# A two-layer graph attention network: folding W2 with the source vector and spreading late scores beside the last blocks

## Chip, cores, metric

One core of a Trainium2 chip. The time is the device time of one execution in microseconds. The kernel before takes 937.47 us, the median of three runs (936.48 to 937.52).

## What is computed

The reference is two graph attention layers over 1250 nodes and 20000 edges (with self loops), a residual and a layer norm. `src` and `dst` are drawn edge lists, so the kernel builds the count matrix of edges on the chip and treats each layer as dense attention with that matrix as weight.

```python
def _gat_layer(x, src, dst, W, a_src, a_dst, bias, concat):
    h = (x @ W).reshape(N, H, C)
    al_s = einsum('nhc,hc->nh', h, a_src)
    al_d = einsum('nhc,hc->nh', h, a_dst)
    e = leaky_relu(al_s[src] + al_d[dst], 0.2)
    m = segment_max(e, dst)
    ex = exp(e - m[dst])
    alpha = ex / (segment_sum(ex, dst)[dst] + 1e-16)
    out = segment_sum(h[src] * alpha[:, :, None], dst)
    ...
h = elu(_gat_layer(x, ..., W1, as1, ad1, b1, concat=True))     # 4 heads of 512
out = _gat_layer(h, ..., W2, as2, ad2, b2, concat=False)       # 1 head, 768
return layernorm(x + out)
```

What matters here: the second layer's source score of a node is the dot product of h2 = hidden x W2 with `as2`. It is also the dot product of the hidden row with the folded vector W2 x as2. And the shift of each target needs the largest source score among its neighbours, so it needs the source scores of all nodes.

## The kernel before

Nodes are in NB = 10 blocks of B = 125. All matrix products are made of three float32r matmuls (high x high, high x low, low x high; the helper `products`, L1722 to L1728), so every operand is split into a high part (ACT, a copy) and a low part (DVE, a subtraction).

Layer one runs over four heads. A head is 20 chunks: two groups g of five target blocks, ten source blocks b each. For each chunk ACT makes relu (`act_relu`, L585), POOL adds the shift row (`pool_add`, L595), ACT makes exp (L610), DVE multiplies by counts (L617), ACT splits off the high part (L623) and DVE the low part (L632), into three slots; TensorE multiplies with the head's hx and hlo (`chunk`, L1851). In the second group of heads 0 to 2 TensorE also makes the next head's block (`make`, L1875), DVE splits it (`split_h`) and makes the masked maxima of the next head, and the next shift goes through DRAM (`store_shift`, L720, `load_grow`, L714). `make(h, b)` waits for the low split of block b - 2. Chunks are numbered through, 0 to 79 in layer one (CHUNKS = 80), 80 to 99 in layer two.

The second projection reads the hidden rows back from DRAM (`hblk`, two slots), transposes each block in two halves of eight 128-column pieces (`transpose_h`, L1840, half n of block n // 2), ACT and DVE split the transposed half (`split_hT`, L1123, L1450), and `mm_half` (L1896) makes 8 steps of six matmuls with W2p, high and low parts of W2 in SBUF. The first half is transposed behind chunk 77, the second behind mm_half(0). ACT evicts each block (`h2_out`), DVE makes its two dot products with as2 and ad2 (`scores2`, L1514), each source score goes through DRAM into the row arow2, and DVE makes the neighbour maxima of the ten target blocks in four pieces: sources 0 to 3 (`maxima2`), then 4 and 5, 6 and 7, 8 and 9 (`part_maxima2`, p = 0 to 2), ten maxima each and a merge.

After the last block the order is written out by hand: last dot products, TensorE spreads the last source score over all partitions (`spread`, L1788, a matmul with a broadcast column against the identity), ten maxima of part 2, merge, the shift of all ten blocks (`dve_shift`, L637), a spread of all target scores (drow2) in between, then the spread of the shift (gcol) in two groups, evictions of these rows, and the chunk loop of layer two, whose low and high parts have ten slots (PT2). TensorE holds the first group's sums of all five target blocks in PSUM (`piece2`, ORDER2), then waits for DVE's first two evictions (`evict2`) and takes the second group target by target. Eviction, norm and store follow block by block on DVE, POOL (rsqrt by pow) and SP. SP's queue issues every DMA, in its program order.

Of the kernel before, what the change touches and what calls it, by code (L numbers as in the profile page):

```python
# [14 lines left out]
F32 = mybir.dt.float32  # L15
# [15 lines left out]
H = 4  # L31
# [68 lines left out]
W2F = 8  # L100

# [21 lines left out]
def gat_kernel(nc, x, src, dst, W1, as1, ad1, b1, W2, as2, ad2, b2, out):  # L123
# [5 lines left out]
    s2_d = nc.dram_tensor("score2_scratch", (NB, B), F32, kind="Internal").ap()  # L129
    hid_d = nc.dram_tensor("hidden_scratch", (N, HID), F32, kind="Internal").ap()  # L130

    with ExitStack() as ctx:
# [103 lines left out]
        pbuf = sb("pbuf", [B, PR, GN], F32)  # L236

# [59 lines left out]
        cursor[0] = tail_at + HID * 4  # L297
        nbp.append(sb("nbp2", [B, NB, QW], BF16))
        cursor[0] = tail_at + 6 * N * 2
        drow2 = sb("drow2", [B, N], F32)  # L300
        pbuf2 = sb("pbuf2", [B, PR, GN], F32)
# [3 lines left out]
        grow2 = sb("grow2", [B, N], F32)  # L305
        xres += [sb(f"xres{i}", [B, D], F32) for i in range(2, GT)]
        assert cursor[0] <= tail_at + 6 * N * 2
# [10 lines left out]
        PT2 = [sb(f"PT2_{i}", [B, 2, GN], F32R) for i in range(3, PR2)] + PT2  # L318
# [88 lines left out]
        d2_sb = sem("d2_sb")  # L407
        g2_sb = sem("g2_sb")
        s2_stored = sem("s2_stored")
        ld_s2 = [sem(f"ld_s2_{i}") for i in range(QP + 1)]  # L410
        h2x_one = sem("h2x_one")
# [20 lines left out]
        h2_sb = sem("h2_sb")  # L432
        al2_done = sem("al2_done")
# [107 lines left out]
        def ht_banks(half):  # L541

            return ((6, 7), (4, 5))[half]
# [29 lines left out]
        def pslot(c):  # L573

            return pbuf[:, c % PR, :] if c < CHUNKS else pbuf2[:, c % PR, :]
# [9 lines left out]
        def act_relu(act, c):  # L585
# [5 lines left out]
            if h < H and b == 0:  # L591
                act.wait_ge(ld_drow[g], RS * (h + 1))
            act.activation(pslot(c), src[:, g * GN:(g + 1) * GN], ACT.Relu, scale=UP, bias=bias).then_inc(z_done, 1)  # L593

        def pool_add(pool, c):  # L595
# [53 lines left out]
        def _(sp):  # L649
# [136 lines left out]

            for h in range(H - 1):
# [1202 lines left out]
```

## Time and profile before

| | |
|---|---|
| median of three runs | 937.47 us |
| the profiled execution | 937.02 us |
| its span | 935.1 us |
| mean granted clock of TensorE | 0.987 |
| PE busy | 881.1 us (94%) |
| DVE busy | 602.1 us (64%) |
| ACT busy | 424.4 us (45%) |
| POOL busy | 198.1 us (21%) |
| HBM traffic | 118 GB/s over the span |

The page of the profile has the busy tenths of each engine in 40 slices of 23.4 us. From slice 9 on TensorE is at 9 or more in all slices but one: the slice from 795 to 818 us, where its busy digit is 6 and its clock digit 7. DVE is near full in layer one and in the last fifth, and at 2 to 4 during the second projection. Busy shares say which engine has room; what sets the end is read from the waits and from the times at which a stage's last steps stand.

### The profile page before, as it was taken

The numbers are of one execution on the slowest core, as the hardware profiler recorded it, in microseconds if no ns is written. First come the engines' busy times: TensorE is split into PE (matmuls) and PEld (weight loads), VectorE is DVE, ScalarE is ACT, GpSimd is POOL, SyncE is SP. The second block draws the span as 40 slices with busy tenths as digits, with TensorE's granted clock in tenths as the row PEclk, the third lists the DMA queues.
The fourth block names the chain that finished last, engine by engine and source line by source line (L and its number), as shares of the span: only waits on it lengthen the run. The fifth ranks groups of instructions, "written<-read, shape, count | busy, mean of one in ns | idle before, by whom it ended". The sixth has DMA issues, their size and how long they took to land.

```text
span 935.1 us, 15156 instructions
## 1 busy us (share of the span) xinstructions
PE 881.1 (94%) x5719; PEld 796.9 (85%) x5719; DVE 602.1 (64%) x1169; ACT 424.4 (45%) x686; POOL 198.1 (21%) x134
## 2 busy tenths in 40 slices
PE   4998879999999999999999999989999999699996
PEld 2455557799888998889988899989999999599996
DVE  9458663668873889638895488672223334497886
ACT  5456452276643866339652396661111111487300
POOL 1000000144212332124321244300000000155452
PEclk9999989999999999999999999999999999799999
DMA  8609999462548237472174243655223322400223
GB/s 298 145 14 132 178 174 159 135 211 81 177 138 239 67 103 212 112 231 78 29 214 139 68 142 117 174 166 115 72 48 70 85 48 30 102 1 2 69 84 95
DMA packets 64450, 111.18 MB, mean 119 GB/s; under 512 B 31772, under 2 KB 33464, under 8 KB 63004
## 3 DMA queue, kind: packets, MB, share of 16 engines
q1 hardware_dynamic: 64379, 110.22, 45.7%
q8 instruction: 46, 0.75, 0.4%
q14 instruction: 25, 0.20, 0.1%
HBM read 85.25 MB, written 24.94 MB: 118 GB/s over the span
## 4 chain that ended last, share of the span: by engine, by line
PE 67%; DVE 11%; issue 9%; POOL 6%; ACT 3%; DMA 2%; DVEq 1%; SPq 1%; POOLq 0%; ACTq 0%
PE ps L1726 19%; PE ps L1728 19%; PE ps L1727 19%; POOL pbuf L608 5%; PE ps L1755 3%; PE ps L1696 2%; PE ps L1847 2%; PE ps L1686 1%; DVE pbuf L621 1%; DVE h2f L1632 1%; DMA mask_scratch<-nbs 1%; DVE h2f L1606 1%; DVE vbuf L1440 1%; DMA w1f<-in_L_gnn_W 1%; DVE bnst L1623 1%
## 5 line engine op out<-in xcount | busy, mean ns | idle before, releaser
L608 POOL TENSOR_TENSOR pbuf<-pbuf,grow 125x625 f32<-125x625 f32 x100 | 169.9, 1700 | 701.2 <-ACT pbuf L593 261.1
L1726 PE MATMUL ps<-hx,PThi 125*125 125x260 f32 (+5 forms) x800 | 227.3, 284 | 3.0 <-DVE vbuf L1441 2.5
L1728 PE MATMUL ps<-hx,PTlo 125*125 125x260 f32 (+5 forms) x800 | 225.4, 282 | 0.0
L1727 PE MATMUL ps<-hlo,PThi 125*125 125x260 f32 (+4 forms) x800 | 224.9, 281 | 0.0
L1726 PEld LDWEIGHTS ps<-hx,PThi 125*125 125x125 f32 x800 | 148.7, 186 | 7.0 <-DVE vbuf L1441 2.9
L1727 PEld LDWEIGHTS ps<-hlo,PThi 125*125 125x125 f32 x800 | 149.1, 186 | 1.4
L1728 PEld LDWEIGHTS ps<-hx,PTlo 125*125 125x125 f32 x800 | 149.0, 186 | 0.0
L1726 PE MATMUL ps<-W2p,hT 128*125 128x384 f32 x320 | 109.7, 343 | 3.2 <-DVE hT L1453 1.7
L1728 PE MATMUL ps<-W2p,hT 128*125 128x384 f32 x320 | 108.1, 338 | 0.0
L1727 PE MATMUL ps<-W2p,hT 128*125 128x384 f32 x320 | 108.1, 338 | 0.0
L621 DVE SCALAR_TENSOR_TENSOR pbuf<-pbuf,counts 125x625 f32<-125x625 f32 x100 | 90.7, 907 | 25.3 <-ACT pbuf L615 25.2
L630 ACT ACTIVATE PThi<-pbuf 125x625 fp32r<-125x625 f32 x80 | 57.8, 722 | 106.1 <-PE ps L1728 57.0
L615 ACT ACTIVATE pbuf<-pbuf,s_sl 125x625 f32<-125x625 f32 x100 | 81.2, 812 | 48.9 <-POOL pbuf L608 48.8
L635 DVE TENSOR_TENSOR PTlo<-pbuf,PThi 125x625 fp32r<-125x625 f32 x80 | 77.1, 964 | 40.4 <-ACT PThi L630 40.2
L1453 DVE TENSOR_TENSOR hT<-ps,hT 128x500 fp32r<-128x500 f32 x40 | 25.2, 672 | 108.7 <-ACT hT L1129 108.7
L1726 PE MATMUL ps<-h2x,PT 125*125 125x384 f32 (+9 forms) x250 | 77.6, 310 | 6.2 <-DVE PT L635 4.2
L1129 ACT ACTIVATE hT<-ps 128x500 fp32r<-128x500 f32 x40 | 21.2, 586 | 133.0 <-PE ps L1847 133.0
L593 ACT ACTIVATE pbuf<-drow,s_up 125x625 f32<-125x625 f32 x100 | 80.2, 804 | 0.0
L1727 PE MATMUL ps<-h2lo,PT 125*125 125x384 f32 (+7 forms) x250 | 77.3, 309 | 0.0
L1728 PE MATMUL ps<-h2x,PT 125*125 125x384 f32 (+9 forms) x250 | 77.3, 309 | 0.0
L1728 PE MATMUL ps<-W1hi,xr 128*125 128x512 f32 x180 | 71.1, 395 | 0.0
L1726 PE MATMUL ps<-W1hi,xr 128*125 128x512 f32 x180 | 71.0, 395 | 0.0
(186 smaller groups left out, 1571.6 us busy)
## 6 DMA issues: line engine op xcount, KB each, us to landing
xr<-xT_scratch SPq DMA_DIRECT2D x30, 750.0 KB, 4.9
nbm<-mask_scratch SPq DMA_DIRECT2D x40, 273.4 KB
hidden_scratch<-vbuf SPq DMA_DIRECT2D x40, 224.0 KB
hblk<-hidden_scratch SPq DMA_DIRECT2D x10, 896.0 KB
xT_scratch<-xa SPq DMA_DIRECT2D x20, 375.0 KB, 11.7
w1f<-in_L_gnn_W SPq DMA_DIRECT2D x12, 512.0 KB, 9.1
w1raw<-in_L_gnn_W SPq DMA_DIRECT2D x4, 1536.0 KB, 7.9
w2raw<-in_L_gnn_W SPq DMA_DIRECT2D x14, 384.0 KB, 5.4
```

Source lines behind the costliest of these rows:

```text
L593: act.activation(pslot(c), src[:, g * GN:(g + 1) * GN], ACT.Relu, scale=UP, bias=bias).then_inc(z_done, 1)
L608: pool.tensor_tensor(pslot(c), pslot(c), src[:, g * GN:(g + 1) * GN], ALU.add).then_inc(e_done, 1)
L615: act.activation(pslot(c), pslot(c), ACT.Exp, scale=SLOPE, bias=bias).then_inc(p_done, 1)
L621: dve.scalar_tensor_tensor(pslot(c), pslot(c), 1.0, C[:, b, g * GN:(g + 1) * GN], ALU.min, ALU.mult).then_inc(pc_done, 1)
L630: act.activation(hi_slot(c), pslot(c), ACT.Copy).then_inc(pt_hi, 1)
L635: dve.tensor_tensor(lo_slot(c), pslot(c), hi_slot(c).bitcast(F32), ALU.subtract).then_inc(pt_lo, 1)
L1129: hi = act.activation(ht_part(n % 2, 0, a), PS[:, bank, 0:4 * B], ACT.Copy)
L1453: lo = dve.tensor_tensor(ht_part(n % 2, 1, a), PS[:, bank, 0:4 * B], ht_part(n % 2, 0, a).bitcast(F32), ALU.subtract)
L1726: pe.matmul(dst, ahi, bhi, start=start, stop=False, skip_group_check=shared)
L1727: pe.matmul(dst[:, 0:n], ahi, blo, start=False, stop=False, skip_group_check=shared)
L1728: return pe.matmul(dst, alo, bhi, start=False, stop=stop, skip_group_check=shared)
L1755: t = pe.matmul(win_bank(w), oh_lo[:, bass.ds(at_slot(first, i, v), 1), :].rearrange("p o n -> p (o n)"), ring[:, w % 2, v, 0:win_cols(w)] ...
```

## The change

The source scores of the last two blocks no longer come from h2. W2 x as2 is computed in layer one: sixteen row blocks of W2 are loaded into one buffer (`load_fold2`) and DVE multiplies each with as2 and sums it (FOLD2: in the second groups of heads 0, 1 and 2, chunks b = 0, 1, 5, 8, 9, in head 2 also 7). The folded vector goes to DRAM and comes back as a row in three pieces (PP: 768, 768, 512 columns); DVE makes the dots of hidden blocks 8 and 9 with it (`late_dots`), in the iterations of blocks 6 and 7, and adds them (`late_scores`).

TensorE spreads the source scores of blocks 7, 8 and 9 in the second half of block 8 (before step LATE_S = 6), so that parts 1 and 2 of the maxima and the shift of targets 0 to 4 are made beside the last two blocks. It spreads that shift in the last half (before step LATE_G = 3). The last block's h2 is evicted behind the first chunk's high split. DVE adds the shift to chunk 80 straight from PSUM; the rows of the target scores (drow2) and of the second group's shift come through DRAM. The first chunk of layer two waits for the banks piece by piece. The slots of PT2 are taken in another order, and `prow`, `nbp2` and `drow2` have other places in SBUF. ACT waits for the last maximum ahead of h2_out(8), and SP's b2row and xres loads stand behind the new row loads.

The second half of the first hidden block is transposed behind chunk 78, with the same banks as the first half, and split ahead of the last group's eviction.

```diff
+PP = ((0, D), (D, 2 * D), (2 * D, HID))
+LATE_S, LATE_G = 6, 3
+FOLD2 = tuple((h, b) for h in range(H - 1) for b in ((0, 1, 5, 8, 9) if h < H - 2 else (0, 1, 5, 7, 8, 9)))
...
+            def load_fold2(h, b):
+                if (h, b) in FOLD2:
+                    i = FOLD2.index((h, b))
+                    if i > 0:
+                        sp.wait_ge(fold2_done, i)
+                    sp.dma_start(wf2[:], W2[128 * i:128 * i + 128, :]).then_inc(ld_fold2, 16)
...
+                load_fold2(h, 0)
                 if h > 0:
                     for t in range(GT):
                         store_hid(NB * h - GT + t)
                 load_drow(h + 1, 0)
+                load_fold2(h, 1)
                 if h + 2 < H:
...
+                    load_fold2(h, (5, None, 7, None, 8)[t])
                 store_shift(h + 1)
                 load_grow(h + 1, 0)
                 load_xr(h + 1, NB - 2)
+                load_fold2(h, 9)
...
+            load_prow(2)
+            sp.wait_ge(ht_ps, 2 * NB - 2)
+            load_part(1)
+            sp.wait_ge(dot_done, 2 * len(PP) + 1)
+            load_part(2)
+            sp.wait_ge(g_stored, RS * H)
+            load_row(drow2, d2_d, 0, ld_drow[0])
+            sp.wait_ge(al2_done, 2 * NB - 2)
+            store_column(d2_d, al2[:, 1, GT:NB], 1)
+            sp.wait_ge(g_done, H + 2)
+            store_column(g2_d, gcol[:, H * NB + GT:(H + 1) * NB], 1)
+            sp.wait_ge(g_stored, RS * (H + 2))
+            load_row(drow2, d2_d, 1, ld_drow[1])
+            load_row(grow2, g2_d, 1, ld_grow[1])
...
             split_hT(0)
+            act.wait_ge(pt_lo, CHUNKS)
+            split_hT(1)
             act.wait_ge(ag, ag_at(CHUNKS - 1))
...
+                    if b == NB - 2:
+                        act.wait_ge(bc2_ps, 1)
+                        act.activation(arow2[:, (NB - 3) * B:N], PS[0:B, 6, 0:3 * B], ACT.Copy).then_inc(bc2_sb, 1)
                     split_hT(2 * b + 3)
-                h2_out(b)
+                if b == NB - 2:
+                    act.wait_ge(mx_last, QP * NB)
+                if b < NB - 1:
+                    h2_out(b)
...
             split_h2(0)
-            shift2_out(0)
-            shift2_out(1)
             act_exp(act, CHUNKS)
+            act.wait_ge(bc2_ps, 2)
+            act.activation(grow2[:, 0:CW], PS[0:B, 4, 0:CW], ACT.Copy)
+            act.activation(grow2[:, CW:GN], PS[0:B, 5, 0:B], ACT.Copy).then_inc(bc2_sb, 1)
+            act_hi(act, CHUNKS)
+            h2_out(NB - 1)
+            act.wait_ge(h2_sb, NB)
+            act_exp(act, CHUNKS + 1)
...
+                if g == 1 and (h, b) in FOLD2:
+                    i = FOLD2.index((h, b))
+                    dve.wait_ge(ld_fold2, RS + 16 * (i + 1))
+                    dve.wait_ge(fold2_done, i)
+                    dve.scalar_tensor_tensor(wf2junk[:], wf2[:], 1.0, as2row[:], ALU.mult, ALU.mult, accum_out=w2a[:, i:i + 1]).then_inc(fold2_done, 1)
...
+            def late_dots(p):
+
+                lo, hi = PP[p]
+                dve.wait_ge(ld_a2, 2 * RS + RS * (p + 1))
+                dve.wait_ge(al2_done, 2 * NB - 6 if p < 2 else 2 * NB - 4)
+                for b in (NB - 2, NB - 1):
...
+                    dve.scalar_tensor_tensor(a2junk[:, 0, 0:hi - lo], hblk[:, b % 2, lo:hi], 1.0, prow[:, 0:hi - lo], ALU.mult, ALU.mult,
+                                             accum_out=dots[:, b - NB + 2, p:p + 1]).then_inc(dot_done, 1)
...
+                split_hT(2 * b + 3)
+                if b == 8:
+                    for m in range(NB):
+                        part_maxima2(2, m)
+                    merge(2)
+                    shift2(0)
                 scores2(b)
+                if b == 6:
+                    late_dots(0)
+                if b == 7:
+                    late_dots(2)
+                    late_scores()
...
+            dve.wait_ge(z_done, CHUNKS + 1)
+            dve.wait_ge(bc2_ps, 2)
+            dve.tensor_tensor(pslot(CHUNKS)[:, 0:CW], pslot(CHUNKS)[:, 0:CW], PS[0:B, 4, 0:CW], ALU.add)
+            dve.tensor_tensor(pslot(CHUNKS)[:, CW:GN], pslot(CHUNKS)[:, CW:GN], PS[0:B, 5, 0:B], ALU.add).then_inc(e_done, 1)
+            split_h2(0)
+            dve_counts(dve, CHUNKS)
+            dve_lo(dve, CHUNKS)
+            scores2(NB - 1)
+            shift2(1)
...
-                if c == CHUNKS - 3:
-                    transpose_h(0)
+                if c in (CHUNKS - 3, CHUNKS - 2):
+                    transpose_h(c - CHUNKS + 3)
...
+                    if n == 2 * NB - 3 and k == LATE_S:
+                        pe.wait_ge(dot_done, 2 * len(PP) + 1)
+                        pe.wait_ge(ht_lo, 2 * NB - 1)
+                        spread(lambda m: al2[:, 0, m:m + 1], lambda m: (6, (m - NB + 3) * B), NB - 3, NB).then_inc(bc2_ps, 1)
+                    if n == 2 * NB - 1 and k == LATE_G:
+                        pe.wait_ge(g_done, H + 1)
+                        spread(lambda m: gcol[:, H * NB + m:H * NB + m + 1], four_from(4), 0, GT).then_inc(bc2_ps, 1)
...
                 for u, order in enumerate(ORDER2):
+                    if c == 0 and u < 2:
+                        pe.wait_ge(h2_sb, NB - 1 + u)
+                    if c == 0 and u == 2:
+                        pe.wait_ge(bc2_sb, 2)
```

## Rows read from the trace of the kernel before

**Rows 1.** Waits of TensorE from 800 us on: us in total, times, longest

```profile
PE ps L1726 <- DVE PT L635: 4.2, 1, 4.2
PE ps L1726 <- DVE h2f L1606: 2.0, 1, 2.0
```

**Rows 2.** Timeline, projection's end and chunk loop: start, length, engine, line, operation

```profile
766.64 0.95 DVE L1520 SCALAR_TENSOR_TENSOR a2junk<-h2f,a2row 125x768 bf16<-125x768 f32 x1
...
781.03 1.02 PE L1847 MATMUL ps<-ident,hblk 125*128 125x125 f32 x8
781.81 0.42 PE L1726 MATMUL ps<-W2p,hT 128*125 128x384 f32 x1
...
798.98 0.81 ACT L1167 ACTIVATE h2f<-ps 125x768 f32<-125x768 f32 x1 [15.12 <-PE ps L1728]
...
812.36 0.82 ACT L615 ACTIVATE pbuf<-pbuf,s_sl 125x625 f32<-125x625 f32 x1
...
815.38 0.80 ACT L593 ACTIVATE pbuf<-drow,s_up 125x625 f32<-125x625 f32 x1
...
815.87 0.55 PE L1726 MATMUL ps<-h2x,PT 125*125 125x256 f32 x1 [4.19 <-DVE PT L635]
...
872.19 0.80 ACT L593 ACTIVATE pbuf<-drow,s_up 125x625 f32<-125x625 f32 x1
```

**Rows 3.** Stretches: length, busy us (xcount) of each engine, PEclk, DMA share, GB/s

```profile
815.80:818.80 3.00, 2.93 (x14) 2.96 (x15) 2.38 (x3) 2.71 (x5) 1.52 (x1) 0.50 0.20 52
818.80:868.00 49.20, 49.20 (x414) 49.20 (x414) 41.67 (x39) 38.70 (x52) 25.60 (x15) 1.00 0.01 1
...
873.20:876.60 3.40, 3.40 (x11) 3.40 (x12) 2.61 (x3) 0.95 (x2) 3.40 (x2) 0.53 0.58 184
```

**Rows 4.** Timeline of TensorE: the spread of ten columns ahead of layer one

```profile
180.33 2.42 PE L1792 MATMUL ps<-ident,gcol 125*125 125x125 f32 x20 [1.04 <-DVE gcol L645]
```

**Rows 5.** Timeline of DVE: first of ten part maxima, and their merge

```profile
786.13 0.41 DVE L1545 CUSTOM_DVE_ANT_0 junk<-nbp,arow 125x250 bf16<-125x250 bf16 x1
...
790.77 0.17 DVE L1553 TENSOR_TENSOR mx<-mx,mxp 125x10 f32<-125x10 f32 x1
```

**Rows 6.** Timeline at the end: DVE's last eviction, TensorE's last matmul

```profile
927.24 0.15 DVE L1594 TENSOR_SCALAR deps<-ps 125x1 f32<-125x1 f32 x1
...
927.41 0.34 PE L1728 MATMUL ps<-h2x,PT 125*125 125x384 f32 x1
```

**Rows 7.** Timeline, layer one's end: transposes, split, eviction, first products of two halves

```profile
601.93 0.27 PE L1847 MATMUL ps<-ident,hblk 125*128 125x125 f32 x1
...
604.13 1.25 DVE L1453 TENSOR_TENSOR hT<-ps,hT 128x500 fp32r<-128x500 f32 x2
608.33 0.16 DVE L1427 TENSOR_SCALAR deps<-ps 125x2 f32<-125x2 f32 x1 [2.94 <-PE ps L1728]
...
611.63 0.44 PE L1726 MATMUL ps<-W2p,hT 128*125 128x384 f32 x1 [1.55 <-DVE vbuf L1441]
...
623.71 0.44 PE L1726 MATMUL ps<-W2p,hT 128*125 128x384 f32 x1 [1.66 <-DVE hT L1453]
```

**Rows 8.** Page's DMA issues, SP's waits, and the timeline in head 1

```profile
w2raw<-in_L_gnn_W SPq DMA_DIRECT2D x14, 384.0 KB, 5.4
...
SPq L717 <- DMA shift_scratch<-gcol: 20.6, 3, 7.5
...
402.87 0.69 DVE L1339 TENSOR_TENSOR hlo<-ps,hx 125x512 fp32r<-125x512 f32 x1 [0.38 <-ACT hx L995]
...
409.52 0.40 PE L1726 MATMUL ps<-W1hi,xr 128*125 128x512 f32 x1
```

**Rows 9.** DVE's W1 split beside POOL and alone; head 1's second group as stretch

```profile
317.98 1.79 DVE L1343 TENSOR_TENSOR W1lo<-w1raw,W1hi 128x512 fp32r<-128x512 f32 x1
...
333.95 0.68 DVE L1343 TENSOR_TENSOR W1lo<-w1raw,W1hi 128x512 fp32r<-128x512 f32 x1
...
344.00:420.00 76.00, 75.79 (x470) 67.44 (x469) 50.18 (x85) 32.37 (x49) 16.60 (x11) 1.00 0.60 171
```

More of the change, by code:

```diff
@@ L236, in gat_kernel @@
         pbuf = sb("pbuf", [B, PR, GN], F32)
+        wf2 = sb("wf2", [128, D], F32)
+        wf2junk = sb("wf2junk", [128, D], BF16)
+        w2a = sb("w2a", [128, KC], F32)
+        cursor[0] = base_attr
+        as2row = sb("as2row", [128, D], F32)
         cursor[0] = base_attr + 2 * (N * 4 + 24)
@@ L317, in gat_kernel @@
         h2lo = sb("h2lo", [B, NB, D], F32R)
-        PT2 = [sb(f"PT2_{i}", [B, 2, GN], F32R) for i in range(3, PR2)] + PT2
+        PT2 = [PT2[2], PT2[1]] + [sb(f"PT2_{i}", [B, 2, GN], F32R) for i in range(3, PR2)] + [PT2[0]]
         assert cursor[0] <= base0 + 2 * KC * D * 4
@@ L539, in h2_banks, with ht_banks @@
             return PS[0:B, 2 * s:2 * s + 2, 0:DH]
-        def ht_banks(half):
-            return ((6, 7), (4, 5))[half]
+        def ht_banks(n):
+            return (4, 5) if n % 2 and n > 1 else (6, 7)
         def ht_part(half, part, a):
@@ L810, in _ @@
                 load_grow(h + 1, 1)
+            sp.wait_ge(fold2_done, KC)
+            for lo, hi in ((0, XP), (XP, 128)):
+                sp.dma_start(w2a_d.rearrange("k p -> p k")[lo:hi, :], w2a[lo:hi, :], allow_slow_non_contiguous=True).then_inc(rows_stored, 16)
             sp.wait_ge(mk_done, H * NB)
@@ L955, in add_bias_late @@
                 pool.tensor_tensor(y[:, n, :], y[:, n, :], b2row[:], ALU.add).then_inc(yb_done, 1)
-            for c in range(CHUNKS, CHUNKS + 2 * NB):
+            pool.wait_ge(e_done, CHUNKS + 1)
+            for c in range(CHUNKS + 1, CHUNKS + 2 * NB):
                 pool_add(pool, c)
@@ L1498, in _ @@
             split_hT(0)
+            split_hT(1)
             evict_group(NG - 1)
@@ L1553, in merge, with late_scores, shift2 @@
                 dve.tensor_tensor(mx[:, lo:hi], mx[:, lo:hi], mxp[:, p * NB:(p + 1) * NB], ALU.max).then_inc(mx_all, 1)
-            for b in range(NB):
-                if b > 0 and b + 1 < NB:
+            dots = bnst[:, 0:2, 0, 0:len(PP)]
+            def late_dots(p):
[3 more added lines that the diff above has]
+                for b in (NB - 2, NB - 1):
+                    if p > 0 or b == NB - 1:
+                        dve.wait_ge(dot_done, 2 * p + b - NB + 2)
+                    if p == 0:
+                        dve.wait_ge(ld_hb[b % 2], RS * (b // 2 + 1))
+                    dve.scalar_tensor_tensor(a2junk[:, 0, 0:hi - lo], hblk[:, b % 2, lo:hi], 1.0, prow[:, 0:hi - lo], ALU.mult, ALU.mult,
+                                             accum_out=dots[:, b - NB + 2, p:p + 1]).then_inc(dot_done, 1)
+            def late_scores():
+                dve.wait_ge(dot_done, 2 * len(PP))
+                dve.tensor_reduce(al2[:, 0, NB - 2:NB], dots, AX.X, ALU.add).then_inc(dot_done, 1)
+            def shift2(g):
+                lo, hi = H * NB + g * GT, H * NB + (g + 1) * GT
+                dcol = al2[:, 1, g * GT:(g + 1) * GT]
+                dve.wait_ge(mx_all, QP)
+                dve.wait_ge(al2_done, (2 * GT, 2 * NB - 2)[g])
+                dve.scalar_tensor_tensor(mneg[:, lo:hi], mx[:, lo:hi], -1.0, dcol, ALU.mult, ALU.subtract).then_inc(m_neg, 1)
+                dve.wait_ge(m_neg, H + 1 + g)
+                dve.scalar_tensor_tensor(negm[:, lo:hi], mneg[:, lo:hi], SLOPE, mneg[:, lo:hi], ALU.mult, ALU.min).then_inc(m_sb, 1)
+                dve.wait_ge(m_sb, H + 1 + g)
+                dve.scalar_tensor_tensor(gcol[:, lo:hi], negm[:, lo:hi], 1 / SLOPE, dcol, ALU.mult, ALU.add).then_inc(g_done, 1)
+            for b in range(NB - 1):
+                if b > 0:
                     split_hT(2 * b + 2)
@@ L1581, in split_h2 @@
                 dve.tensor_tensor(h2lo[:, b, :], h2f[:, b, :], h2x[:, b, 0:D].bitcast(F32), ALU.subtract).then_inc(h2_lo, 1)
-            for b in range(NB):
-                part_maxima2(2, b)
-            merge(2)
-            dve_shift(dve, H, al2[:, 1, :])
+            dve.wait_ge(z_done, CHUNKS + 1)
[7 more added lines that the diff above has]
+            shift2(1)
             def evict2(n):
```

157 lines of the change are left out of this document (75 added, 82 removed).

## The prediction

> **What bounds the kernel now.** I read the waits of TensorE first, then the timeline where the long ones lie. Behind the prologue TensorE waits only in short spots; the expensive one is the seam between the second projection (h2 = hidden x W2) and the second attention [rows 1, 2]. There the eviction of the last product begins at 798.98 us and the first product of the attention at 815.87: 16.9 us. In between everything stands in one line: h2 eviction, dot products of the last block, spread of its source score, ten maxima, shift, two more spreads, their evictions, then add, exp, counts and split of the first chunk. Behind the gap TensorE's clock stands at 0.50, 1.2 of 2.4 GHz, for 3.0 us: 14 matmuls there, where the stretch behind has 414 in 49.2 us (0.119 each) [rows 3]. That is 1.3 us more.
>
> The second thing to see is that TensorE isn't what ends the kernel behind that seam. One loop of ACT, POOL and DVE prepares twenty chunks: relu, add, exp, counts, split. The relu of the third (chunk 82) begins at 815.38 and that of the last at 872.19, seventeen steps of 3.34 us on average. TensorE catches up with it and waits 2.0 us for DVE's first evictions [rows 1, 2]. DVE reaches the last eviction at 927.24, when TensorE has its last matmul at 927.41 [rows 6]. So the end gains what **the relu of chunk 82** gains, not what TensorE's first matmul gains.
>
> **Part 1, the seam to the attention.** From it go the dot products of the last source score, twenty maxima, the first shift, the spread of drow2 and half of the last spread. They go beside the last blocks, if these are in time. I place them on the clock of before.
>
> Source scores of blocks 8 and 9 come from hidden rows times the folded W2, on DVE in 768 + 768 + 512 columns. The last two of these dots follow the passes of block 7, whose second ran from 766.64 to 767.6 [rows 2]: plus 2 x 0.65 (an estimate by columns from 0.95 us for 768) plus 0.2, 769. TensorE asks for them at step 6 of the last half but two. A half takes (798.8 - 781.81)/2 = 8.5 us, a step 1.06, so that half starts at 781.03 - 8.5 = 772.5 and the step at 778.9. Margin 10 us; the loads of the folded row must land inside it (a W2 block of like size lands in 5.4 us [rows 8]). No cost.
>
> Spreads inside the projection: ten columns took 20 matmuls and 2.42 us at full clock [rows 4], so three columns cost 0.7 us and five 1.15. The product stream is full, so these 1.85 us are on TensorE's path.
>
> Maxima: the early spread ends at 779.7, ACT evicts it by 780.3, DVE goes on some 0.5 later, 780.8. Ten maxima took 786.13 to 790.77 [rows 5], 4.65 us. First ten and merge to 785.7, the hT split (1.25) to 786.9, second ten and merge to 791.8, three steps of the shift to 792.5. The hT split is now queued behind ten maxima; the last half wants it at 791, so nobody waits. TensorE wants gcol at step 3 of the last half: 781.81 + 0.7 + 8.5 + 3.2 = 794.2. **Margin 1.7 us**, the thinnest of all. ACT stands meanwhile in front of h2_out(8), which waits for the last maximum; behind it are queued two relus, which take 1.6 us and are wanted at 795.4. Then: spread done 795.4, DVE's add out of PSUM (two pieces, 0.9) to 796.3. From this exp to TensorE's first product took 812.36 to 815.87 [rows 2], 3.5 us: 799.8. The projection ends at 800.8. So TensorE goes on without a gap at full clock, and gains 16.9 - 1.85 + 1.3 = 16.4 us itself.
>
> The engines' loop gains less, for h2_out(9) can't begin before TensorE is done: 798.98 + 1.85 = 800.83 to 801.65. Behind it on ACT come the exp of chunk 81 and then the relu of 82, at 802.4 in place of 815.38: 13.0 us. DVE has scores2(9) and the second shift ahead of its counts of chunk 81 (801.7 to 803.4), which leaves the next relu 12.8 early. Chunk 81 is ready at 806.6 and TensorE done with chunk 80 (45 matmuls by 0.119) at 806.0, so it waits 0.6. From there the loop is that of before. The rows of targets 5 to 9 now go through DRAM: stored at 804, seen at most 7.5 us later [rows 8], the rows issued by 814 and in some five microseconds there, wanted by the relu of chunk 90 at 802.4 + 8 x 3.34 = 829. SP's loads of b2row and xres are queued behind them and are wanted only by the evictions ahead of the second group. Free. TensorE's surplus is given back there: it waits some 5 us, not 2.0. Its clock fell behind the 2.0 already (0.53 from 873.2 to 876.6 [rows 3]), so that costs the same again or up to 1 us more. Part 1: **-12.8 us**, bounds -15 (the loop runs at its fastest steps) and -9 (both margins missed by 2).
>
> **Part 2, the first block's second half.** TensorE now stops 1.55 us for evictions at 611.63 and 1.66 us for hT at 623.71 [rows 7]. Eight transposes take 781.81 - 781.03 = 0.78 us. They go ahead of the last chunk of layer one, which starts at 606.3 (610.1, where the wait began, less 30 x 0.119 and the tail of a matmul). From such transposes at 601.93 to the end of DVE's split at 605.38 it took 3.45 us, so this split ends at 609.75, and evict_group, queued behind it, begins 1.4 us after its 608.33 [rows 7]. First half 613.0 to 621.5, eight transposes, second half at 622.3 in place of 623.71. The late W2 splits are queued behind on DVE and wanted 1.4 us earlier than now; where they miss it, tenths are lost. **-1.3 us** (bounds -1.7 and 0).
>
> **Part 3, the fold in layer one.** Sixteen loads of 384 KB, and sixteen passes of DVE over 768 columns at 0.95, in the second groups of three heads. TensorE is full there and DVE one to two chunks ahead. It counts when DVE must be back: the make of block 8 wants the hlo split that began at 402.87 and ended at 403.56, and starts at 409.52 [rows 8], slack 5.9. Fold 0 adds 0.9. Fold 1 waits for a load that SP issues only when fold 0 is done, 5.4 us: some 4.9 late, of which I take off 0.8 for a pass of ACT for which DVE waits there anyway. Fold 5 adds 0.9, and the shift's store stands 1 us behind a W2 load: 6.0 of 5.9 used in heads 0 and 1. In head 2 SP also waits for fold 7 ahead of that store, 1.5 more. So TensorE stalls 0.1 twice and 1.4 once. I take **+1.5 us** (bounds 0 and +11). The store of w2a (2048 elements of 4 bytes) has 16 us until W2 is loaded. Free.
>
> What a fold costs beside POOL: a W1 split of 512 columns takes 0.68 alone and 1.79 beside POOL's add [rows 9], 1.1 more. I don't count that: POOL works 16.6 of the 76 us of such a stretch [rows 9]. The Trainium skill (SBUF — State Buffer, Who interferes with whom) says that a DVE instruction with two inputs in SBUF and a GpSimd instruction that reads SBUF can't run together; the one that comes second waits for the whole of the other. By that rule, the trace agrees; rival (c) is what it would do if it met every fold.
>
> **Sum.** The profiled execution took 937.02 us, 0.45 under the median. 937.02 - 12.8 - 1.3 + 1.5 = 924.4; on the median's footing 924.9.
>
> **The rivals.** (a) The loop isn't the bound and the end follows TensorE: 16.4 - 0.6 + 1.3 - 1.5 = 15.6, so 921.9, and 920.4 with no stall in layer one. Against it: the 2.0 us wait and DVE's late last eviction. 0.10. (b) The late scores miss TensorE: each microsecond past the 1.7 of margin is one of TensorE idle in its last half. If the maxima come 4 us later than placed, 2.3 are lost, and a clock fall may add 1.3: 928.5. 0.13. (c) Each of the three folds ahead of the shift meets a POOL add, 3 x 1.1 = 3.3 per head: 3.4 + 3.4 + 4.7 = 11.5 in place of 1.5, 934.9; half of it, 930. 0.10. (d) **Slower**: the W2 loads land late behind xr, masks and w1raw, so that the hlo split is late by more than 5.9. At 12 us late it is 6.1 in each head, 18.3 against 14.1: 941.7. It turns slower from 5.9 + 14.1/3 = 10.6 us late. For it speaks a DMA share of 0.60 there [rows 9], against it the 5.4 of a W2 block. 0.04. (e) The seam isn't emptied: something the early spread needs comes only with the last block, the maxima stay serial, and parts 2 and 3 alone remain: 937.7. 0.03. My forecast has 0.60, its own range 922 to 928.
>
> A measurement can tell 0.2%, 1.9 us. Faster by more: 0.92; within: 0.03; slower: 0.05. The range takes in (a), (b) and half of (c): 920 to 931.
>
> **What would show it.** Spreads of 6 and 10 matmuls inside the last three halves; no gap of TensorE over 1 us at the end of the projection, and clock 1.00 through it; a wait of about 5 us for DVE's h2f before the second group; a wait for hlo in the makes of head 2 and hardly elsewhere. Wrong if TensorE waits on gcol or on the dots inside the projection, if the last chunk of layer one ends more than 3 us later, or if the loop of twenty chunks runs at another rate than 3.34.

## The result, and the profile after

The changed kernel takes 925.04 us (median of 4 runs, 922.75 to 926.22) against 936.98 (936.31 to 937.52): a ratio of 0.9859, 95% interval 0.9838 to 0.988, 11.9 us faster. The profiled execution took 924.97 (span 922.9), where the forecast's sum for it was 924.4. On the page of the profile the slice from 795 to 818 us, the low one of before, is full now. Two slices of the page before that stand under 9 as well weren't named ahead of the prediction: that from 608 to 631 us (digit 8), where the two waits of part 2 lie, and the last (6).

First the waits of TensorE behind 190 us: in total, times, longest. The 4.2 us wait for PT of [rows 1] is gone, none for gcol or for the late scores has come, and the wait ahead of the second group (h2f) has grown from 2.0 to 5.6.

```profile
PE ps L1831 <- DVE h2f L1712: 5.6, 1, 5.6
PE ps L1831 <- DVE vbuf L1495: 4.3, 7, 2.1
PE ps L1831 <- DVE PT L650: 0.6, 1, 0.6
```

Then the timeline of the new seam (start, length, engine, line, operation), for [rows 2].

```profile
764.53 0.96 DVE L1627 SCALAR_TENSOR_TENSOR a2junk<-hblk,prow 125x768 bf16<-125x768 f32 x1 [4.84 <-DMA prow<-folded_scratch]
...
772.74 0.16 DVE L1633 TENSOR_REDUCE al<-bnst 125x2 f32<-125x6 f32 x1
778.92 0.82 PE L1897 MATMUL ps<-ident,al 125*125 125x125 f32 x6
779.77 0.49 ACT L1254 ACTIVATE arow<-ps 125x375 f32<-125x375 f32 x1 [5.92 <-PE ps L1897]
...
791.71 0.17 DVE L1645 SCALAR_TENSOR_TENSOR gcol<-negm,al 125x5 f32<-125x5 f32 x1
794.15 1.25 PE L1897 MATMUL ps<-ident,gcol 125*125 125x125 f32 x10
...
798.88 1.37 DVE L650 TENSOR_TENSOR PT<-pbuf,PT 125x625 fp32r<-125x625 f32 x1 [0.80 <-ACT PT L645]
800.50 0.28 PE L1831 MATMUL ps<-h2x,PT 125*125 125x256 f32 x1
800.70 0.81 ACT L1228 ACTIVATE h2f<-ps 125x768 f32<-125x768 f32 x1 [1.85 <-PE ps L1833]
801.55 0.82 ACT L630 ACTIVATE pbuf<-pbuf,s_sl 125x625 f32<-125x625 f32 x1
802.27 0.81 ACT L608 ACTIVATE pbuf<-drow,s_up 125x625 f32<-125x625 f32 x1
...
806.64 0.38 PE L1831 MATMUL ps<-h2x,PT 125*125 125x256 f32 x1 [0.60 <-DVE PT L650]
```

The late dots end at 772.9 and TensorE takes them at 778.92; gcol is there at 791.9 and taken at 794.15, a margin of 2.3 us. TensorE goes from the projection to the attention without a gap. The relu of chunk 82, at 815.38 in [rows 2], begins at 802.27: 13.1 us earlier, forecast 13.0. What comes before it in the execution (prologue, layer one, the way to block 1) differs by only 0.1 us in sum, so the two times can be compared as they stand.

To see where all the time went I cut the profiled executions at four points of TensorE's timeline: its spread ahead of layer one [rows 4], the end of the last product of layer one, the first product of block 1's first half, the end of the last product of the projection. The last column runs from there to the end of the span. The other kernels are those of the experiments.

| kernel | prologue | layer one | to block 1 | projection | to the end |
|---|---|---|---|---|---|
| before | 180.3 | 429.7 | 22.9 | 165.9 | 136.1 |
| changed | 181.9 | 430.3 | 20.8 | 167.7 | 122.2 |
| changed, again (e0) | 177.9 | 430.3 | 20.7 | 167.7 | 122.2 |
| transposition alone (e1) | 181.2 | 430.6 | 20.7 | 165.9 | 136.9 |
| folds alone (e2) | 182.6 | 429.5 | 23.0 | 165.9 | 136.5 |
| no transposition move (e3) | 182.7 | 429.5 | 23.0 | 167.7 | 122.2 |
| late spread (e4) | 179.1 | 430.4 | 20.7 | 171.3 | 122.3 |
| ACT order (e5) | 183.6 | 430.4 | 20.7 | 167.7 | 121.5 |
| extra matmuls (e6) | 183.3 | 430.4 | 20.7 | 167.7 | 122.4 |
| early evictions (e7) | 181.7 | 430.4 | 20.7 | 167.7 | 121.8 |
| folds tripled (e8) | 183.0 | 445.0 | 20.7 | 167.7 | 122.3 |
| early, filled (e10) | 184.0 | 430.3 | 20.8 | 167.7 | 121.0 |
| relu ahead (e12) | 181.3 | 430.3 | 20.7 | 167.7 | 124.5 |
| POOL held (e13) | 183.0 | 430.3 | 20.7 | 167.7 | 118.9 |

Changed less before: +1.6 +0.6 -2.1 +1.8 -13.9 = -12.0, within rounding of the spans' 12.2. The table shows something else: the stages repeat within some tenths, and what scatters between executions is the prologue (177.9 to 184.0). So I compare stages, and take medians for the whole.

### The profile page after: what moved, and what is told of

The parts are those of the page before. It is cut to its first block, busy times and chain, and to the rows that moved or that the text cites. A ratio compares the mean times of both kernels' runs of the same rounds, so it can differ in the third digit from the quotient of the medians.

```text
span 922.9 us, 15201 instructions
## 1 busy us (share of the span) xinstructions
PE 873.8 (95%) x5693; PEld 790.9 (86%) x5693; DVE 621.3 (67%) x1215; ACT 422.2 (46%) x681; POOL 205.4 (22%) x133
## 4 chain that ended last, share of the span: by engine, by line
PE 69%; DVE 10%; issue 9%; POOL 6%; ACT 3%; DMA 1%; DVEq 0%; SPq 0%; POOLq 0%; ACTq 0%
PE ps L1831 19%; PE ps L1833 19%; PE ps L1832 19%; POOL pbuf L623 6%; PE ps L1860 4%; PE ps L1801 2%; PE ps L1952 2%; PE ps L1791 1%; DVE h2f L1738 1%; DVE pbuf L636 1%; DVE h2f L1712 1%; DMA w1f<-in_L_gnn_W 1%; DVE bnst L1729 1%; DVE vbuf L1495 1%; DVE vbuf L1494 1%
## 5 line engine op out<-in xcount | busy, mean ns | idle before, releaser
L623 POOL TENSOR_TENSOR pbuf<-pbuf,grow 125x625 f32<-125x625 f32 x99 | 177.4, 1793 | 680.9 <-ACT pbuf L608 244.3
L636 DVE SCALAR_TENSOR_TENSOR pbuf<-pbuf,counts 125x625 f32<-125x625 f32 x100 | 87.1, 871 | 29.4 <-ACT pbuf L630 29.2
L645 ACT ACTIVATE PThi<-pbuf 125x625 fp32r<-125x625 f32 x80 | 57.8, 722 | 107.2 <-DVE pbuf L636 65.2
L650 DVE TENSOR_TENSOR PTlo<-pbuf,PThi 125x625 fp32r<-125x625 f32 x80 | 84.4, 1055 | 28.2 <-ACT PThi L645 28.2
```

Source lines behind the costliest of these rows:

```text
L623: pool.tensor_tensor(pslot(c), pslot(c), src[:, g * GN:(g + 1) * GN], ALU.add).then_inc(e_done, 1)
L636: dve.scalar_tensor_tensor(pslot(c), pslot(c), 1.0, C[:, b, g * GN:(g + 1) * GN], ALU.min, ALU.mult).then_inc(pc_done, 1)
L645: act.activation(hi_slot(c), pslot(c), ACT.Copy).then_inc(pt_hi, 1)
L650: dve.tensor_tensor(lo_slot(c), pslot(c), hi_slot(c).bitcast(F32), ALU.subtract).then_inc(pt_lo, 1)
```

## The experiments

**The parts one by one.** e0 is the changed kernel again. e1 is the kernel before with the order of transposes, hT splits and their banks of part 2 (excerpt; the wait for `v_done` moves behind `mm_half(1)`):

```diff
-                if c == CHUNKS - 3:
-                    transpose_h(0)
+                if c in (CHUNKS - 3, CHUNKS - 2):
+                    transpose_h(c - CHUNKS + 3)
...
-                if b == 0:
-                    pe.wait_ge(v_done, H * NB)
-                    transpose_h(1)
```

e2 is the kernel before with the folds (excerpt):

```diff
+                if g == 1 and (h, b) in FOLD2:
+                    i = FOLD2.index((h, b))
+                    dve.wait_ge(ld_fold2, RS + 16 * (i + 1))
+                    dve.scalar_tensor_tensor(wf2junk[:], wf2[:], 1.0, as2row[:], ALU.mult, ALU.mult, accum_out=w2a[:, i:i + 1]).then_inc(fold2_done, 1)
...
+                load_fold2(h, 0)
+                load_fold2(h, 1)
```

e3 is the changed kernel with the first diff taken back.

> The changed kernel once more, unchanged, for how far its runs scatter and whether the 1.6 us by which layer one began later is part of the change. If it belongs to the change (more transfers queued in the prologue), TensorE's spread ahead of layer one begins near 181.9 us again, against 180.3; if it is scatter, it begins anywhere between 180 and 182 here and in the other kernels. Ratio to the kernel before: 0.986 to 0.987.

> The kernel before with part 2 alone: the first block's second half transposed behind the last chunk but one of layer one. Prediction: -1.3 us (bounds -1.7 and 0), ratio 0.9986; the profile shows the second half of block 0 following the first with no wait for hT, and the eight transposes (0.78) ahead of the last chunk. The rival 'it only moves the wait': the first half starts later by as much as the second no longer waits, ratio 1.000.

> The kernel before with part 3 alone: the sixteen loads of W2, the sixteen passes of DVE and the store of the folded column; their result is not used by anything. Two semaphores are shared to make room. The prediction had +1.5 us (TensorE stalls 0.1, 0.1, 1.4 for hlo), ratio 1.0016. The trace of the changed kernel shows no such stall and the splits back with 5.3, 4.4 and 1.25 us to spare, so the theory now is 0, ratio 1.000. If the folds cost TensorE something by shared ports or DMA all the same, layer one is longer by 1 us or more with no wait for hlo.

> The changed kernel without part 2: folds and the emptied seam, with the first block's second half transposed behind its first half as before. If the parts add up, this is 1.3 us slower than the changed kernel and 12.8 less what the folds cost faster than the kernel before: ratio 0.987 to 0.9885. The difference to the kernel with the folds alone is part 1 by itself: -12.8 by the prediction (bounds -15 and -9). If part 1 depends on where block 0 ends, the parts don't add up and the difference to the changed kernel is not 1.3.

All four shared 23 runs of the kernel before, median 938.54.

| kernel | median us | ratio to before | 95% interval |
|---|---|---|---|
| e0 | 924.82 | 0.9863 | 0.984 to 0.9886 |
| e1 | 936.27 | 0.9982 | 0.9966 to 0.9998 |
| e2 | 938.64 | 0.9998 | 0.9981 to 1.0016 |
| e3 | 925.83 | 0.9861 | 0.9838 to 0.9884 |

The prologue is scatter, and wider than the 180 to 182 that I expected: 177.9 in e0, the same kernel that had 181.9. Part 2 reads from the stages as (430.6 - 429.7) + (20.7 - 22.9) = -1.3 in e1 and (430.3 - 429.5) + (20.8 - 23.0) = -1.4 between e3 and the changed kernel. Part 3 costs layer one nothing: 429.5 in e2 and e3, 429.7 before. Part 1 is +1.8 in the projection and -14.3 behind it (136.5, the mean of before, e1 and e2, to 122.2): -12.5. By stages the parts add up; the ratios of e0 and e3 alone (0.9863 and 0.9861) couldn't tell the 1.4 us of part 2. The edits of part 1 (late scores, the order of the seam, the slots of PT2, the places of the buffers) were measured only together.

The timeline of TensorE in the changed kernel shows part 2 at work at the two places of [rows 7]; e1 has the same. The wait for evictions is 0.6 longer, the wait for hT ahead of the second half is gone.

```profile
614.38 0.44 PE L1831 MATMUL ps<-W2p,hT 128*125 128x384 f32 x1 [2.12 <-DVE vbuf L1495]
623.71 0.42 PE L1831 MATMUL ps<-W2p,hT 128*125 128x384 f32 x1
```

**How much room the folds have.** e8 does each fold pass three times.

```diff
+                    for j in range(2):
+                        dve.wait_ge(fold2_done, 3 * i + j)
+                        dve.scalar_tensor_tensor(wf2junk[:], wf2[:], 1.0, as2row[:], ALU.mult, ALU.mult, accum_out=w2a[:, i:i + 1]).then_inc(fold2_done, 1)
```

> The changed kernel with each of the sixteen fold passes of layer one done three times, one behind the other (1.9 to 2.1 us more each on DVE; the following loads of W2 come later by as much, too). By the slack read in the trace of the changed kernel (5.3, 4.4 and 1.25 us in the three heads between the hlo split and the make that wants it; three or four folds stand ahead of it, so 6 or 8 us more) TensorE stalls by 0.7 to 1, 1.6 to 2 and 7: layer one 9 to 10 us longer, 1.010. If the slack isn't what limits (DVE catches up elsewhere, the loads overlap), under 5. If folds cost TensorE also outside these makes, over 12.

Median 939.43, ratio to before 1.0024 (1.0002 to 1.0045); layer one 445.0, 14.7 longer. The timeline of TensorE in e8 has four stalls for hlo:

```profile
253.88 0.50 PE L1834 MATMUL ps<-W1hi,xr 128*125 128x512 f32 x1 [2.36 <-DVE hlo L1393]
370.95 0.50 PE L1834 MATMUL ps<-W1hi,xr 128*125 128x512 f32 x1 [2.57 <-DVE hlo L1393]
489.38 0.49 PE L1834 MATMUL ps<-W1hi,xr 128*125 128x512 f32 x1 [2.37 <-DVE hlo L1393]
539.60 0.79 PE L1834 MATMUL ps<-W1hi,xr 128*125 128x512 f32 x1 [3.28 <-DVE hlo L1393]
```

Three of them are not where I looked. They stand at the make of block 2, behind folds 0 and 1. In the changed kernel (DVE, then TensorE) that place has little room, in head 0 250.32 - 249.03 = 1.3 us:

```profile
248.35 0.68 DVE L1393 TENSOR_TENSOR hlo<-ps,hx 125x512 fp32r<-125x512 f32 x1
...
250.32 0.39 PE L1831 MATMUL ps<-W1hi,xr 128*125 128x512 f32 x1
```

In heads 1 and 2 it is 0.9 and 1.4 there, and in the kernel before it was 4.2 to 4.5 in all three: less than the 5.9 of block 8 on which the prediction worked. In e8 the split of head 0 came 3.7 us later against TensorE's start of the stage (253.14 - 182.98, against 248.35 - 181.93), and 3.7 - 1.3 = 2.4 is the stall. The fourth is the make of block 8 in head 2, the last with folds, which has 1.25 us of room in the changed kernel; there I had expected 7 us and it was 3.28. The waits are 10.6 us in sum; two of the makes behind them took 5.98 us instead of 4.35 at a clock that fell (granted 0.83 and 0.85 in the ten microseconds behind the waits), 3.3 more. The remaining 0.8 isn't accounted for. My 9 to 10 had the waits nearly right in sum but in the wrong places, which is luck, and left the clock out. With folds three times as long the whole gain of the seam is gone.

**Rival (b), the margin of the shift.** e4 spreads the late scores four steps later.

```diff
-                    if n == 2 * NB - 3 and k == LATE_S:
+                    if n == 2 * NB - 2 and k == 2:
```

> The changed kernel with the spread of the three late rows four steps later on TensorE (step 2 of the next half in place of step 6: 4 x 1.06 and the transposes of 0.8 between, 4.2 to 5 us). The margin of the target's shift was read as 2.3 us (the shift at 791.9, wanted by TensorE's spread at 794.2). If that margin is real and the price of a miss is one for one (rival b), TensorE waits 1.9 to 2.7 us in its last half and the end is 2 to 2.7 later than the changed kernel, up to 1.3 more if the clock falls behind the wait. If there is more slack than read (the chain behind the spread runs faster when it is late), under 1 us.

Median 927.49, ratio 0.9894 (0.9865 to 0.9922); projection 3.6 longer, the rest as before. TensorE's timeline:

```profile
770.46 0.45 PE L1831 MATMUL ps<-W2p,hT 128*125 128x384 f32 x1 [0.45 <-DVE hT L1507]
...
789.64 0.44 PE L1831 MATMUL ps<-W2p,hT 128*125 128x384 f32 x1 [0.50 <-DVE hT L1507]
794.99 1.35 PE L1897 MATMUL ps<-ident,gcol 125*125 125x125 f32 x10 [1.90 <-DVE gcol L1645]
```

The maxima now end later than the margin allows, and TensorE waits 1.9 us for gcol; the hT split queued behind the ten maxima holds it 0.5 more. The wait at 770.46 is ahead of the edit and not its doing: in this execution DVE waited 6.0 us for the folded row, 4.8 in the changed kernel, and the hT split is queued behind the dots. Over these three waits (2.85 us together) TensorE falls 3.6 us behind the changed kernel, so each costs 0.2 to 0.3 us more than its length. The two that the edit made cost 2.9, somewhat more than the 2 to 2.7 that I expected. No clock fall followed. So a miss costs a little more than one for one, without the fall of the clock that rival (b) had in it, and the margin is real. The late folded row shows one more margin: it made TensorE wait at 770.46, some 8 us ahead of the place where the changed kernel asks for the dots (778.92). What is queued behind a late pass can be wanted sooner than the pass itself.

**Rival (a), does the end follow TensorE?** e6 gives TensorE 35 more matmuls ahead of chunk 85.

```diff
+                if c == 5:
+                    for _ in range(35):
+                        pe.matmul(PS[0:B, 7, BANK - 240:BANK], PT2[5][:, 0, 0:B], h2x[:, 5, 0:240], start=False, stop=False, skip_group_check=True)
```

> The changed kernel with 35 more matmuls of 240 columns ahead of the products of chunk 85, into columns of PSUM that nothing reads: 35 x 0.1 = 3.5 us more for TensorE behind the seam. If the loop of ACT, POOL and DVE sets the end (forecast), TensorE's wait of 5.6 us ahead of the second group shrinks to about 2 and the end doesn't move (the clock may even fall less: up to 1 us earlier). If TensorE's own progress sets it (rival a), the end is 3.5 later. Counted from the end of the projection, 115.6 in the one case and 119.1 in the other.

Median 923.67, ratio 0.9838 (0.9817 to 0.986). From the projection to the end of the span 122.4, against 122.2: 3.5 us of work cost nothing. TensorE's wait ahead of the second group:

```profile
862.23 0.44 PE L1831 MATMUL ps<-h2x,PT 125*125 125x384 f32 x1 [1.72 <-DVE h2f L1712]
```

Its last product came 2.3 us earlier than in the changed kernel (113.3 against 115.6 us behind the projection), for the clock didn't fall behind the short wait. Stretches of the changed kernel, then of e6 (length, PE, PEld, DVE, ACT, POOL, clock, DMA share, GB/s):

```profile
860.90:864.60 3.70, 3.70 (x12) 3.70 (x13) 3.70 (x2) 0.00 (x0) 3.70 (x3) 0.50 0.53 164
```

```profile
862.00:866.00 4.00, 3.77 (x21) 3.77 (x22) 4.00 (x3) 0.00 (x0) 4.00 (x3) 1.00 0.55 174
```

12 matmuls in 3.7 us at 1.2 GHz, 21 in 4.0 at 2.4. Even so the end stayed. So (a) falls, and more than that: a faster TensorE gains nothing in the second group either. What counts is DVE. In the changed kernel its waits from 857 us on name no TensorE:

```profile
DVE h2f L1738 <- POOL rstd L1007: 6.6, 10, 0.7
DVE PT L650 <- ACT PT L645: 1.6, 2, 0.8
DVE pbuf L636 <- ACT pbuf L630: 0.2, 1, 0.2
```

From DVE's first eviction (857.59) to the end of the span are 65.3 us. It is 65.2 in the kernel before (869.87 to 935.1), and 65.2 to 65.5 in e0 to e6, e8 and e12, whatever TensorE's clock was. DVE is busy for 52.5 of these 65.3 us; 8.4 are the waits above, 6.6 of them for POOL's rstd ahead of the ten normalisations, 3.2 come behind its last pass, and the rest are short gaps. TensorE has little to spare, though. In the changed kernel its last matmul and DVE's last eviction stand so:

```profile
915.93 0.33 PE L1833 MATMUL ps<-h2x,PT 125*125 125x384 f32 x1
916.59 0.60 DVE L1712 SCALAR_TENSOR_TENSOR h2f<-ps,rden,xres 125x384 f32<-125x384 f32 x1
```

The room is 0.3 us. That a TensorE later than this would set the end was not tried.

**What sets the loop's step.** e5 moves ACT's exp and relu and DVE's counts ahead of the last steps of the seam; e12 also does each relu three chunks ahead.

```diff
             act_hi(act, CHUNKS)
+            act_exp(act, CHUNKS + 1)
             h2_out(NB - 1)
+            act_relu(act, CHUNKS + 2)
             act.wait_ge(h2_sb, NB)
-            act_exp(act, CHUNKS + 1)
...
             dve_lo(dve, CHUNKS)
+            dve_counts(dve, CHUNKS + 1)
             scores2(NB - 1)
```

> The changed kernel with three steps moved ahead of the last ones of the seam: on ACT the exp of chunk 81 ahead of the last h2 eviction and the relu of chunk 82 right behind it, on DVE the counts of chunk 81 ahead of the last score pass. Theory: the loop behind the seam sets the end, and it starts with the relu of chunk 82; the eviction, exp and relu take 0.8 each, so the relu comes 0.8 earlier, and chunk 81 is ready 1.7 earlier. The gain that passes on is that of the relu, 0.8, up to 1.7: 0.9982 to 0.9991 of the changed kernel, 923.3 to 924.2. If ACT isn't in the loop's path: 0.

> As the one before, and ACT does each relu three chunks ahead of its exp in place of two. Two theories on what sets the loop's step (3.65 us in the first ten chunks, 3.0 in the second ten). Dependency theory: POOL's add (2.0), exp (0.8) and relu (0.8) stand in one circle of 3.6, since ACT does the relu behind the exp and POOL waits for it; with the relu ahead the step falls toward ACT's own 3.0 in the first group and TensorE (45 matmuls by 0.119 a chunk is 5.4, then the wait ahead of the second group is gone) sets the end: 3 to 5 us faster than the one before. Sharing theory: POOL's add (1.3 alone) and DVE's counts, lo split and h2 split (0.75 + 0.75 + 0.9) exclude one another and add to 3.65: the step stays, 0 to 1 us.

e5: median 924.8, ratio 0.9851 (0.9832 to 0.9871). The relu of chunk 82 begins 0.74 us behind the projection instead of 1.60, the evictions 56.1 instead of 56.9, the end 121.5 instead of 122.2. What the relu gains the end gains, 0.7 to 0.8, and not the 1.7 of chunk 81. e12: median 925.72, ratio 0.9859 (0.9837 to 0.9881), end 124.5, 3.0 later than e5. Neither theory had it slower. ACT's timeline in e12 names the reason:

```profile
825.23 0.82 ACT L608 ACTIVATE pbuf<-drow,s_up 125x625 f32<-125x625 f32 x1 [0.88 <-DVE PT L650]
```

A relu three chunks ahead writes the buffer that DVE's split has only just left (pbuf has three), so DVE's split stands in one line with ACT and POOL, and the step is 3.8 to 4.0 in the first group. With three buffers two chunks ahead was the better of the two orders.

For the changed kernel the dependency theory's circle holds. POOL's timeline there, in the first and in the second group:

```profile
806.69 2.01 POOL L623 TENSOR_TENSOR pbuf<-pbuf,grow 125x625 f32<-125x625 f32 x1 [1.64 <-ACT pbuf L608]
810.34 2.02 POOL L623 TENSOR_TENSOR pbuf<-pbuf,grow 125x625 f32<-125x625 f32 x1 [1.64 <-ACT pbuf L608]
...
839.06 1.29 POOL L623 TENSOR_TENSOR pbuf<-pbuf,grow 125x625 f32<-125x625 f32 x1 [1.64 <-ACT pbuf L608]
842.00 1.54 POOL L623 TENSOR_TENSOR pbuf<-pbuf,grow 125x625 f32<-125x625 f32 x1 [1.64 <-ACT pbuf L608]
```

From 806.69 on POOL waits 1.64 us for ACT's exp and relu ahead of every add of the loop, so the step is 1.64 plus the length of the add: 3.65 where the add takes 2.0, and 2.9 to 3.2 where it takes 1.29 to 1.54. The sharing of POOL and DVE comes in by that length. In e12 the adds from the third on took 1.29 to 1.54, and the wait ahead of them 2.47 in the first group.

**Towards a better kernel.** DVE does its first two evictions at chunk 97, 56.9 us behind the projection, when TensorE has been done with its first group for 2.5 us. e7 does them one chunk earlier; e10 is e7 with e5's order and 20 matmuls that fill TensorE's wait; e13 is e10 with POOL's bias adds held.

```diff
-                if c == CHUNKS + 2 * NB - 3:
+                if c == CHUNKS + 2 * NB - 4:
                     evict2(0)
...
+                    if c == NB - 1 and u == GT - 1:
+                        for _ in range(20):
+                            pe.matmul(PS[0:B, 7, BANK - 240:BANK], h2x[:, 9, 0:B], h2x[:, 9, 0:240], start=False, stop=False, skip_group_check=True)
...
             pool.wait_ge(ld_b2, RS)
+            pool.wait_ge(pt_lo, CHUNKS + 2 * NB)
             add_bias_late(0)
```

> The changed kernel with DVE's first two evictions behind the seam one chunk earlier in its queue (ahead of the split of chunk 96 in place of 97), nothing else. They began 56.9 us behind the end of the projection in all three looks, while TensorE had its first group done at 54.4 and waited 5.6 us. Theory: DVE's place of these evictions ends the wait. They begin at 53.8 to 54, TensorE's wait is 2.6 to 3 and the end 2.7 to 3 earlier, up to 2.3 more where the clock doesn't fall: ratio to the changed kernel 0.9945 to 0.997. Rival: the splits of chunks 97 to 99 come 3 us later than now and TensorE waits for these in the second group: 0 to 1 us gained.

> The changed kernel with the earlier evictions, the three steps of the ACT order run moved ahead (0.8 us earlier there), and 20 matmuls of 240 columns (2.0 us) into unread columns of PSUM ahead of the last target's products of chunk 89, which keep TensorE at work while it would wait. Theory: wait under 1 us, clock 1.00 behind it, the second group starts 56 to 57 us behind the end of the projection and takes 53.1 as in the run with extra matmuls (55.4 in the changed kernel, whose clock stood at 0.50 for 3.9 us): end at 109.5 to 110.5 against 115.6, ratio to the changed kernel 0.994. Rival: the late splits of chunks 97 to 99 hold TensorE up and the filled time is lost: no better than the early evictions alone.

> The early, filled version with POOL's first two bias adds of the second group (4.8 us, right behind its last add of the loop) held until DVE has done the split of chunk 99. There DVE's counts of chunk 99 took 2.15 us and the split 1.54 beside them, against 0.80 each alone, and TensorE waited 1.9 us for that split and then ran at a lower clock. Sharing theory: both passes take 0.8, the split is done 2.1 earlier, TensorE's wait and the second clock fall go, the second group takes 53.1: 109.5 to 110.5 from the end of the projection, 3 us less than in the early, filled version (113.4). If the passes were long for another reason, they stay and so does the wait: 113.4; if the bias adds are wanted earlier than thought, the norms behind them come later and the tail grows beyond 113.4.

| kernel | median us | ratio to before | 95% interval | to the end |
|---|---|---|---|---|
| e7 | 923.44 | 0.9835 | 0.9808 to 0.9861 | 121.8 |
| e10 | 923.47 | 0.9837 | 0.9811 to 0.9863 | 121.0 |
| e13 | 921.20 | 0.9818 | 0.9787 to 0.9849 | 118.9 |

In e7 TensorE's wait fell from 5.6 to 2.5 and its last product came 2.7 us earlier (112.9 behind the projection), just as expected, yet the end of the span only 0.4. The rival I had named isn't the reason either: TensorE waited 0.4 for the last split. DVE's queue holds the same work in another order. e10 adds e5's 0.8 and nothing for the filled wait: TensorE's last product came 113.4 us behind the projection and not 109.5 to 110.5, for TensorE waited 1.94 for the last split, as its rival had it, and the clock fell (0.66 in the 4 us behind). Only e13 takes work from DVE. The counts and the split of chunk 99 in e10 and in e13:

```profile
866.12 2.15 DVE L636 SCALAR_TENSOR_TENSOR pbuf<-pbuf,counts 125x625 f32<-125x625 f32 x1 [0.22 <-ACT pbuf L630]
869.07 1.54 DVE L650 TENSOR_TENSOR PT<-pbuf,PT 125x625 fp32r<-125x625 f32 x1 [0.80 <-ACT PT L645]
```

```profile
865.03 0.81 DVE L636 SCALAR_TENSOR_TENSOR pbuf<-pbuf,counts 125x625 f32<-125x625 f32 x1 [0.22 <-ACT pbuf L630]
866.64 0.81 DVE L650 TENSOR_TENSOR PT<-pbuf,PT 125x625 fp32r<-125x625 f32 x1 [0.80 <-ACT PT L645]
```

(2.15 - 0.81) + (1.54 - 0.81) = 2.1, and the end is 2.1 earlier (121.0 to 118.9). Cause and size agree. The hold was tried only on top of e10's edits. The Trainium skill (SBUF — State Buffer, Who interferes with whom) says that a DVE instruction with two SBUF inputs and a GpSimd one that reads SBUF lock each other out; by that rule, the pair of rows agrees. My 3 us counted on TensorE's clock as well, which isn't on the path: TensorE's last product did come 3.5 us earlier. e13 is 3.3 us ahead of the changed kernel from the projection to the end, and at 0.9818 the fastest here; the interval of its ratio overlaps that of the changed kernel (0.984 to 0.9886 in e0) slightly.

## Why the prediction was right

The forecast was 924.9, the result 925.04. Point by point:

- *The end gains what the relu of chunk 82 gains.* Right but for the loop's step. It came 13.1 us earlier (13.0). e5 moved the same relu by 0.8 and the end by 0.7; e6 loaded TensorE and the end stayed.
- *Part 1, -12.8.* Measured -12.1 between the two profiled executions and -12.5 by the means. Projection +1.8, as worked out. Counted from the end of the projection the relu gained 14.8 us (16.4 to 1.6) and the end 13.9. The rest went in the loop, which I had going on as before: from the relu of chunk 82 to the first eviction it took 55.3 us (802.27 to 857.59) and not 54.5 (815.38 to 869.87), 3.38 a step and not 3.34. Of POOL's ten adds from 803.15 on, eight took 1.9 us or more, of the ten that answer to them in the kernel before five; by POOL's timeline the step is the add plus 1.64.
- *TensorE goes on without a gap.* Right, with 2.3 us of margin for 1.7 forecast. The dots ended at 772.9, not 769: DVE waited 6.0 us for the hidden block and 4.8 for the folded row, which was seen 7.5 us after SP issued it (757.07 to 764.53), not the 5.4 of [rows 8]. The 10 us of room took it.
- *TensorE's surplus is given back, 5 us of wait.* Right (5.6), with a clock of 0.50 behind it for 3.7 us. That this costs up to 1 us was wrong: TensorE isn't on the path there. I had named DVE's late last eviction as evidence [rows 6], but took the chain only to the evictions. From there on it is DVE's own queue, 65.3 us long.
- *Part 2, -1.3.* Measured -1.3 and -1.4.
- *Part 3, +1.5.* Wrong: nothing, and the wait for hlo in head 2, named as a sign, didn't come. Two terms failed. A fold's load came faster than its price: 3.3 us from issue (348.7) to the pass (352.00) in head 1, and 4.4 us is the page's median for the sixteen, where I took 5.4. And the waits didn't pile up ahead of the shift's store: the splits wanted by the make of block 8 came with 5.3, 4.4 and 1.25 us to spare. The working has a slip as well: 6.0 plus 1.5 less 5.9 is 1.6 for head 2, where it says 1.4. I also watched the wrong place: e8 shows the make of block 2 giving way in each head, with 4.2 us of room before and 0.9 at the least after.
- *Rival (c)*, POOL's sharing on folds: passes of 0.95 to 1.69 us show that it happens, once or twice a head and not three times, and e2 that it costs nothing. *Rival (d)*: DVE waited 2.3 us at most for a W2 block. e8 shows the second half of (d), late splits and a slower kernel, by folds three times as long and not by late loads; late loads themselves were not tried.

That the total was hit to 0.1 us is partly luck: the prologue of the profiled execution was 1.6 us longer than that of the kernel before, by scatter, and this filled the place of the 1.5 of part 3. On the medians of e0 and of the kernel before beside it the change is worth 938.54 - 924.82 = 13.7 us, 1.1 more than the 12.6 of the forecast.

## What to carry to other kernels

Follow the chain past the wait that you remove to the very end of the span: here it ran over ACT's relu, POOL's add and then DVE's queue, and neither a wait of 5.6 us nor a clock fall of TensorE behind the seam cost anything. If an engine's queue is the bound, moving its steps about gains little (0.4 us in e7, where 2.7 were expected); less work on it does, and the first to look for are its passes that run beside a POOL instruction. Where work is put beside other work, list the slack at each point where the engine is awaited, not only at the one that looks tightest; and cut executions into stages before comparing them, since one scattering stage can hide or fake an effect of 2 us.

## What the runs showed of the hardware

DVE's normalisation of 768 columns, with one tensor input, took 2.19 us beside POOL's adds and 0.68 alone, in the changed kernel:

```profile
880.72 2.19 DVE L1738 TENSOR_SCALAR h2f<-h2f,mv,rstd 125x768 f32<-125x768 f32 x1 [0.67 <-POOL rstd L1007]
...
914.48 0.68 DVE L1738 TENSOR_SCALAR h2f<-h2f,mv,rstd 125x768 f32<-125x768 f32 x1 [0.66 <-POOL rstd L1007]
```

POOL began its bias adds at 880.65; at 914.48 it had just ended its rstd and ran nothing beside the pass. I expected this for passes with two inputs only. The Trainium skill (SBUF — State Buffer, Who interferes with whom) names tensor-scalar operations among those of DVE that can take the ports it shares with GpSimd; by that rule, the pair of rows agrees. Seven of the nine whole passes took 2.19 or 2.20, each beside a bias add. At 1.5 us each that is 10.6 us in DVE's queue, which e13 leaves there; to take them away wasn't tried.

A wait of 1.72 us left TensorE's clock at 1.00 (e6), and so did 2.36 and 2.37 us in layer one of e8. 2.57 and 3.28 us there brought it down, and so did the 1.99 of the kernel before [rows 3], the 1.94 of e10 (0.66 in the 4 us behind) and the 2.52 of e7 (0.70). The length of the wait alone doesn't decide it.
